# A Mamba block and a mixture of experts on one core: the row numbers of a routed tile's scatter are copied at the end of that tile's work

## The chip, the core and the metric

The kernel runs on one core of a Trainium2 chip. Its engines work side by side and wait for each other by semaphores: TensorE (matmuls, PE in the profile), VectorE (DVE), ScalarE (ACT), GpSimd (POOL) and SyncE (SP, which issues DMAs). The metric is the device time of one execution in microseconds (us).

## What is computed

A state-space block is added to x, and then a mixture of experts. Only the second matters here:

```python
scores = softmax(x @ gate_w.T)                 # 2048 tokens, 16 experts
topk_w, topk_ids = lax.top_k(scores, TOP_K)    # TOP_K = 6
topk_w = topk_w / (topk_w.sum(-1, keepdims=True) + 1e-20)
...
def body(acc, ew):
    w13_e, w2_e, c_e = ew
    y = _swiglu(x, w13_e, w2_e)
    return (acc + c_e[:, None] * y, None)
out, _ = lax.scan(body, jnp.zeros_like(x), (w13, w2, combine.T))
out = out + _swiglu(x, sw13, sw2)              # the shared expert, for all tokens
```

`_swiglu(x, w13, w2)` is `silu(x @ g.T) * (x @ u.T) @ w2.T` with 512 columns of x and 352 columns inside. Everything is float32.

## The kernel before

The work comes in two parts. Up to about 500 us the state-space block runs; then the experts' tiles follow, 128 tokens each. The first 32 tiles (`NS`) are the shared expert's, in two halves, with tokens in their own order. From tile 32 on come the routed tiles: the tokens of one expert are gathered from a table in HBM, worked on, weighted and added to the output rows by an indirect DMA with addition, a scatter. In the profiled execution there are 104 of them, tiles 32 to 135, for 16 experts. Most of them run in a loop of four tiles per turn (`Fori`), each of which has one of four slots.

A float32 matmul is made of three: every operand is split in a high part (rounded) and a low part (the rest), and high x high, high x low and low x high are summed. So a tile `t` passes through these steps, with the names of the tiles in SBUF:

- GpSimd gathers its rows into `xt` by the numbers in `gid`; SyncE sends them through HBM (`token_quarters`, `xs`), VectorE turns them into a PSUM bank (L1432).
- ScalarE writes the high part `xh` (L911), VectorE the low part `xl` (L1439, function `x_low`); TensorE multiplies both with the expert's weights (`up`, L1794 and L1795).
- ScalarE makes the silu `sg`, VectorE `am`, the product with the token's weight (L1479, `multiply`). TensorE transposes `am` (L1805, three matmuls per tile, which run between the two halves of the next tile's `up`), ScalarE writes `ah` (L921), VectorE `al` (L1485), and TensorE multiplies with the second weights (`down`, L1814).
- ScalarE copies the result to `ys` (L927), and GpSimd issues the scatter `out_x<-ys,aid` (L1074), which reads `ys` and the row numbers in `aid`.

Row numbers move through three small tiles of four columns, one per slot: `gid` (for the gather, written seven tiles ahead, L1456), `mid` (L1462, `keep_ids`, three tiles ahead) and `aid` (for the scatter, L1468, `add_ids`). Each is a copy of 128 x 1 int32 on VectorE. `add_ids` of a tile waits, by `added` of its slot, until the scatter of the tile four earlier has landed, since that one reads the same column.

When an expert begins, both ScalarE and VectorE write the high part of a later expert's weights, ScalarE then issues the load of the next raw weights, and GpSimd writes the low part in one subtraction (L1046), behind which its next scatters stand. Each engine runs its instructions in the order in which the program gives them; no scheduler moves them.

Of the kernel before, what the change touches and what calls it, by code (L numbers as in the profile page):

```python
# [54 lines left out]
NS = 2 * TT  # L55
# [180 lines left out]
def mamba_moe(nc, x, ctxT, g_x, g_f, inT, convw, convb, xpT, dtwT, dtb, alog, dvec,  # L236
# [13 lines left out]
    with ExitStack() as ctx:  # L250
        def alloc(stack, name, shape, dt=F32):
            return stack.enter_context(nc.sbuf_tensor(name, shape, dt))
# [27 lines left out]
        place = alloc(ctx, "place", [P, E, HALF])  # L280
# [218 lines left out]
        def at_least(eng, s, v):  # L499

            if isinstance(v, int) and v <= 0:
                return
            eng.wait_ge(s, v)
# [3 lines left out]
        def apart(eng, s, v, who):  # L507

            at_least(eng, s, v)
            if not isinstance(v, int):  # L510
                eng.sem_inc(waited[who], 1)

        def through(t, s):

            return 16 * (t // 4 + 1) if isinstance(t, int) else 4 * t + 16 - 4 * s
# [31 lines left out]
        def tiles_but_12(eng):  # L547
            return eng.value_load(fours[0:1, 1:2], min_val=NS + E - 12, max_val=TILES - 12)
# [4 lines left out]
        def up_banks(t, s):  # L553

            return misc if isinstance(t, int) and t == 0 else banks[2 * s:2 * s + 2]
# [20 lines left out]
        def _(sp):  # L576
# [28 lines left out]
            def xproj(q, _):  # L605
                bank, m = use("xproj", 0, q)
                apart(sp, gone[bank], m + 1, "sp")
                sp.dma_start(c_d[bass.ds(q, 1)].rearrange("a n t -> (a n) t"), xd[CP:CP + DS, :]).then_inc(cd_stored, 16)
# [535 lines left out]
        def _(dve):  # L1144
# [283 lines left out]
            def turn(t, s4, m=None):  # L1428

                of_slot(dve, moved[s4], t, m, "dve")  # L1430
                dve.wait_ge(xh_done, t - 1)
                nc.vector.transpose(banks[4 + 2 * (s4 % 2)][:].rearrange("p (b r g) -> p g b r", g=G, r=Q),  # L1432
                                    xs[:, s4, :].rearrange("p (g b c) -> p g b c", g=G, c=Q)).then_inc(xt_turned, 1)

            def x_low(t, s):
                dve.wait_ge(xh_done, t + 1)
                at_least(dve, up_done, t - 1)
                source = xt[:, t % 4, 0:H] if isinstance(t, int) and t < NS else banks[4 + 2 * s][:]
                nc.vector.tensor_tensor(xl[:, s, :], source, xh[:, s, :], ALU.subtract).then_inc(xl_done, 1)  # L1439

            def plan_of(t):

                word = dve.value_load(meta[0:1, 1, bass.ds(t, 1)], min_val=0, max_val=NX * (NX + 1) * NR - 1)
                return dve.snap(word % NX), dve.snap(word // NX % (NX + 1)), dve.snap(word // (NX * (NX + 1)))

            def take_weight(t, s4, number, m=None):

                rows_in(dve, t, s4, m, "dve")
                at_least(dve, am_done, t - 3)
                nc.vector.tensor_copy(cc[:, s4:s4 + 1], xt[:, s4, bass.ds(H - 1 + number, 1)]).then_inc(cc_done, 1)  # L1450
# [4 lines left out]
            def gather_ids(t, s4, column=None):  # L1455
                nc.vector.tensor_copy(gid[:, s4:s4 + 1], lists[:, bass.ds(ids_column(t) if column is None else column, 1)]).then_inc(gid_done, 1)  # L1456

            def keep_ids(t, s4):

                apart(dve, gid_done, t + 1, "dve")  # L1460
                apart(dve, aid_done, t - 3, "dve")
                nc.vector.tensor_copy(mid[:, s4:s4 + 1], gid[:, s4:s4 + 1]).then_inc(mid_done, 1)  # L1462

            def add_ids(t, s4):

                apart(dve, mid_done, t + 1, "dve")
                apart(dve, added[s4], through(t - 4, s4), "dve")
                nc.vector.tensor_copy(aid[:, s4:s4 + 1], mid[:, s4:s4 + 1]).then_inc(aid_done, 1)  # L1468

            def multiply(t, s4):  # L1470
                s = s4 % 2
                dve.wait_ge(sg_done, t + 1)
                if isinstance(t, int) and t < NS:
                    weight = share_w[:, 0:1]
                else:
                    dve.wait_ge(cc_done, t + 1)
                    weight = cc[:, s4:s4 + 1]
                at_least(dve, am_turned, t - 1)
                nc.vector.scalar_tensor_tensor(out=am[:, s, 0:I], in0=sg[:, s, :], scalar=weight,  # L1479
                                               in1=up_banks(t, s)[1][:, 0:I], op0=ALU.mult, op1=ALU.mult).then_inc(am_done, 1)  # L1480

            def a_low(t, s):
                dve.wait_ge(ah_done, t + 1)
                at_least(dve, down_done, t - 1)
                nc.vector.tensor_tensor(al[:, s, :], banks[5][:, 0:IP], ah[:, s, :], ALU.subtract).then_inc(al_done, 1)  # L1485
# [11 lines left out]
            def next_weights(t, e):  # L1497

                with dve.If(e > 0):
                    apart(dve, raw_in, raws_of(e), "dve")  # L1500
                    apart(dve, down_done, t, "dve")
                    nc.vector.tensor_copy(w[:, bass.ds((e % 2) * 2 * WCOLS + WCOLS - SHARE, SHARE)],
                                          raws[:, bass.ds((e % 2) * FAR + WCOLS - SHARE, SHARE)]).then_inc(wh_done, 1)

            def beside(work, t):
                for kind, i in work.get(t, ()):
                    if kind == "x2":
                        x2_(NB - 1, i)
                    elif kind == "stats2":
                        stats2(NB - 1, i)  # L1510
                    elif kind == "nmr":
                        nmr_(NB, i)
                    elif kind == "rank":
                        rank_tokens(i // 3, i % 3)
                    elif kind == "place":
                        place_tokens(i % 2)
                    elif kind == "match":
                        match_choices(i // 2, i % 2)
                    elif kind == "gate2":
                        gate(NB - 2, i)  # L1520
                    elif kind == "gate3":
                        gate(NB - 1, i)
                    elif kind == "low":
                        low_piece(i // EARLY, i % EARLY)
                    elif kind == "count":
                        count_tiles(i)
                    elif kind == "experts":
                        number_experts(i)
                    elif kind == "tiles":
                        number_tiles(i)  # L1530
                    else:
                        fill_table(i)

            def tile(t, place, m=None, takes=True, gathers=True):

                def slot_of(d):
                    return (place + d) % 4

                def group_of(d):
                    return None if m is None else m + (place + d) // 4  # L1540

                s, static = place % 2, isinstance(t, int)
                plain = static and t + TAKEN < NS
                if not plain:
                    split, number, column = plan_of(t)
                if not static or t + 1 >= NS:
                    turn(t + 1, slot_of(1), group_of(1))
                a_low(t - 1, 1 - s)
                if static:
                    beside(DVE_AFTER_A, t)  # L1550
                if takes and not plain:
                    take_weight(t + TAKEN, slot_of(TAKEN), number, group_of(TAKEN))
                    keep_ids(t + TAKEN, slot_of(TAKEN))
                if not static or t + 1 >= NS:
                    add_ids(t + 1, slot_of(1))
                if static and t < NS:
                    for late in FIRST_ROWS.get(t, ()):
                        if late >= NS + 4:
                            dve.wait_ge(mid_done, late - 3)
                        gather_ids(late, late % 4)  # L1560
                elif gathers:
                    apart(dve, mid_done, t + TAKEN + 1, "dve")
                    gather_ids(t + AHEAD, slot_of(AHEAD), column)
                x_low(t + 1, 1 - s)
                multiply(t, place % 4)
                if not static or t >= PEELED:
                    next_weights(t, split)

# [31 lines left out]
            last = tiles_but_12(dve) + 11  # L1600
            for k in range(4):
                tile(last - 4 + k, 3 + k, looped, k < 2, False)
            a_low(last - 1, 0)
            multiply(last, 3)
            a_low(last, 1)


# [312 lines left out]
```

## Time and profile before

| | |
|---|---|
| Median of 3 runs | 1419.17 us (1418.41 to 1422.58) |
| Profiled execution, its own time | 1422.3 us |
| Its span, first to last instruction | 1420.5 us |
| TensorE, busy | 1307.5 us |
| GpSimd, busy | 944.7 us |
| VectorE, busy | 851.5 us |
| ScalarE, busy | 729.5 us |

The span is what the trace covers; the execution's own time is 1.8 us more. Busy times are sums over the whole span, in which the two parts of the kernel lean on different engines, so they don't say what bounds the routed tiles; the rows further down are therefore mostly of the routed tiles alone.

### The profile page before, as it was taken

The page shows a single profiled execution, that of the slowest core. Times are in us where ns is not written, and L with a number is a line of the kernel's source. Part 1 is how long each engine was busy: PE and PEld are TensorE (multiplying, and loading weights), DVE is VectorE, ACT ScalarE, POOL GpSimd, SP SyncE. Part 2 cuts the span into 40 slices and gives each one's busy share as a digit, 9 for nine tenths or more (in the row PEclk, how much of TensorE's full clock was granted, in tenths as well). Part 3 has the DMA queues.
Part 4 walks back from the last instruction along what each step waited for, and adds up shares of the span by engine and source line. Part 5 has one row for each costly group of instructions (what it writes and reads, how often), then busy time and mean ns, then how long its engine had stood idle before and what let it go on. Part 6 is the DMA issues. An engine that isn't in the chain of part 4 may idle for free.

```text
span 1420.5 us, 31069 instructions
## 1 busy us (share of the span) xinstructions
PE 1307.5 (92%) x8064; PEld 1175.1 (83%) x8065; DVE 851.5 (60%) x1570; ACT 729.5 (51%) x1317; POOL 944.7 (67%) x671
## 2 busy tenths in 40 slices
PE   7897998998988899999789999999999999999995
PEld 2676887887888789999678988888988898888895
DVE  5879888897989865653244444444444445444441
ACT  5898887988879554343233333333333333333331
POOL 0589898999888847888366556666556665556722
PEclk8899999998999999999999999999999999999999
DMA  4121122223242555655487878887878778877752
GB/s 138 34 73 38 54 68 97 68 68 97 69 130 61 145 142 105 141 100 129 92 246 209 213 185 214 219 213 210 216 181 220 214 199 221 210 191 212 203 134 37
DMA packets 136276, 205.91 MB, mean 145 GB/s; under 512 B 20496, under 2 KB 74384, under 8 KB 134016
## 3 DMA queue, kind: packets, MB, share of 16 engines
q1 hardware_dynamic: 101744, 102.33, 23.8%
q0 software_dynamic: 31024, 62.10, 23.6%
q10 hardware_dynamic: 3440, 40.63, 8.1%
q8 instruction: 36, 0.59, 0.2%
q14 instruction: 32, 0.26, 0.1%
HBM read 130.99 MB, written 76.25 MB: 146 GB/s over the span
## 4 chain that ended last, share of the span: by engine, by line
PE 33%; POOL 12%; issue 9%; DMA 8%; DVE 4%; ACT 2%; POOLq 1%; ACTq 1%; DVEq 0%
PE bank L1814 11%; PE bank L1794 9%; PE bank L1795 9%; DMA out_x<-ys,aid 7%; POOL token_lists L1086 6%; POOL w L1046 4%; PE bank L1805 2%; POOL out_x L1068 1%; DVE hs L1236 1%; ACT w L876 1%; PE bank L1704 1%; PE bank L1690 1%; DVE xl L1439 1%; DMA out_x<-ys 1%; POOLq L1091 1%
## 5 line engine op out<-in xcount | busy, mean ns | idle before, releaser
L1794 PE MATMUL bank<-w,xh 128*128 (+1 forms) x1088 | 365.3, 337 | 26.0 <-DVE xl L1439 24.5
L1008 POOL TENSOR_TENSOR hc<-hs,crow 128x512 f32<-128x512 f32 x254 | 322.1, 1302 | 91.8 <-DVE hs L1236 86.2
L1795 PE MATMUL bank<-w,xh 128*128 (+1 forms) x1088 | 351.3, 323 | 0.0
L1074 POOL DMA_INDIRECT out_x<-ys,aid x104 | 165.2, 1589 | 254.6 <-issue 226.4
L1236 DVE TENSOR_TENSOR_SCAN hs<-dA,bank 128x512 f32<-128x512 f32 x256 | 295.7, 1208 | 50.3 <-PE bank L1704 31.6
L1814 PE MATMUL bank<-w,ah 128*128 (+1 forms) x816 | 259.3, 399 | 15.3 <-DVE al L1485 15.3
L1485 DVE TENSOR_TENSOR al<-bank,ah 128x384 fp32r<-128x384 f32 x136 | 75.8, 558 | 294.9 <-ACT ah L921 279.7
L1794 PEld LDWEIGHTS bank<-w,xh 128*128 128x128 f32 x1088 | 204.7, 188 | 42.5 <-issue 34.3
L927 ACT COPY ys<-bank 128x512 f32<-128x512 f32 x136 | 79.9, 587 | 262.8 <-PE bank L1814 262.8
L1795 PEld LDWEIGHTS bank<-w,xh 128*128 128x128 f32 x1088 | 206.7, 190 | 4.5
L1814 PEld LDWEIGHTS bank<-w,ah 128*128 128x128 f32 x816 | 150.2, 189 | 44.0 <-issue 12.9
L1795 PE MATMUL bank<-w,xl 128*128 (+1 forms) x544 | 176.0, 323 | 0.0
L1794 PE MATMUL bank<-w,xl 128*128 (+1 forms) x544 | 175.9, 323 | 0.0
L921 ACT CAST ah<-bank 128x384 fp32r<-128x384 f32 x136 | 65.2, 480 | 210.7 <-PE bank L1805 210.3
L1690 PE MATMUL bank<-ident,hc 128*128 128x128 f32 x1024 | 161.4, 282 | 7.3 <-POOL hc L1008 4.7
L1704 PE MATMUL bank<-bdiag,duT 128*128 128x128 f32 x1024 | 164.5, 285 | 0.0
L840 ACT ACTIVATE dA<-delta,aneg 128x512 f32<-128x512 f32 x256 | 164.2, 711 | 0.0
L1814 PE MATMUL bank<-w,al 128*128 (+1 forms) x408 | 161.3, 395 | 0.0
L1046 POOL TENSOR_TENSOR w<-raws,w x15 | 144.1, 9608 | 0.4
L1704 PEld LDWEIGHTS bank<-bdiag,duT 128*128 128x128 f32 x1024 | 143.1, 202 | 0.0
L1690 PEld LDWEIGHTS bank<-ident,hc 128*128 128x128 f32 x1024 | 125.6, 146 | 9.9 <-POOL hc L1008 6.1
L1702 PE MATMUL bank<-ident,gt 128*128 128x128 f32 x512 | 107.5, 293 | 26.4 <-DVE hs L1236 21.9
(184 smaller groups left out, 1983.6 us busy)
## 6 DMA issues: line engine op xcount, KB each, us to landing
raws<-in_wall ACTq DMA_DIRECT2D x16, 2176.0 KB, 8.9
token_quarters<-xt SPq DMA_DIRECT2D x104, 256.0 KB
xs<-token_quarters SPq DMA_DIRECT2D x104, 256.0 KB, 3.2
crow<-c_rows SPq DMA_DIRECT2D x64, 256.0 KB, 3.3
xt<-token_rows_turned SPq DMA_DIRECT2D x32, 256.0 KB, 2.9
out_x<-ys POOLq DMA_DIRECT2D x32, 256.0 KB, 4.2
token_rows<-rowb SPq DMA_DIRECT2D x4, 1028.0 KB, 5.9
xrow<-in_x SPq DMA_DIRECT2D x4, 1024.0 KB, 8.0
```

Of the source, the lines that this page charges most:

```text
L840: nc.scalar.activation(dA[:, 4 * (n % 2) + j, :], delta[b % 2][:, j, :], ACT.Exp, scale=aneg[:, j, n:n + 1]).then_inc(dA_done, 1)
L1008: nc.gpsimd.tensor_tensor(hc[:, j, :], hs[:, j, :], crow[:, n % 4, :], ALU.mult).then_inc(hc_done, 1)
L1046: nc.gpsimd.tensor_tensor(columns(w, at + WCOLS, WCOLS), raws[:, raw_at(e)], columns(w, at, WCOLS), ALU.subtract).then_inc(wl_done, 1)
L1074: pool.indirect_dma_start(out_rows, bass.IndirectOffsetOnAxis(ap=aid[:, s:s + 1], axis=0), ys[:, s, :], None, bounds_check=TOKENS - 1, oob ...
L1086: pool.indirect_dma_start(list_d[:, :], bass.IndirectOffsetOnAxis(ap=posi[:, c:c + 1], axis=0), ids[:, chunk:chunk + 1], None).then_inc(li ...
L1236: nc.vector.tensor_tensor_scan(hs[:, j, :], dA[:, 4 * (n % 2) + j, :], dbu[j % 2][:], 0.0, ALU.mult, ALU.add).then_inc(scanned, 1)
L1690: mm = nc.tensor.matmul(ysum[t][:, cols], hc[:, j, t * P:(t + 1) * P], ident[:], start=n == 0 and j == 0, stop=n == DS - 1, is_transpose=T ...
L1702: mm = nc.tensor.transpose(dbu[j % 2][:, t * P:(t + 1) * P], gt[:, n % 2, t, j * P:(j + 1) * P], ident[:])
L1704: mm = nc.tensor.matmul(dbu[j % 2][:, t * P:(t + 1) * P], duT[b % 2][:, t, j * P:(j + 1) * P], bdiag[:, n % 2, t - COPIED, :], start=True, ...
L1794: nc.tensor.matmul(gate_bank[:, 0:I], xx, columns(w, off + ww + k * 2 * I, I), start=first, stop=last)
L1795: mm = nc.tensor.matmul(up_bank[:, 0:I], xx, columns(w, off + ww + k * 2 * I + I, I), start=first, stop=last)
L1814: mm = nc.tensor.matmul(banks[7][:], aa, columns(w, off + ww + W2AT + k * H, H), start=k == 0 and n == 0, stop=k == IK - 1 and n == 2)
```

## The change

`add_ids` is called in another place. Before, the iteration for tile `t` copied the numbers of tile `t + 1`, between `keep_ids` and `gather_ids`, ahead of `x_low(t + 1)`. Now it copies those of its own tile `t`, behind `multiply(t)`, and ahead of `next_weights(t)`. The function itself is the same, with the same waits.

```diff
                 if takes and not plain:
                     take_weight(t + TAKEN, slot_of(TAKEN), number, group_of(TAKEN))
                     keep_ids(t + TAKEN, slot_of(TAKEN))
-                if not static or t + 1 >= NS:
-                    add_ids(t + 1, slot_of(1))
                 if static and t < NS:
...
                     gather_ids(t + AHEAD, slot_of(AHEAD), column)
                 x_low(t + 1, 1 - s)
                 multiply(t, place % 4)
+                if not static or t >= NS:
+                    add_ids(t, place % 4)
                 if not static or t >= PEELED:
                     next_weights(t, split)
...
             a_low(last - 1, 0)
             multiply(last, 3)
+            add_ids(last, 3)
             a_low(last, 1)
```

On VectorE, one tile's iteration in the loop before the change, from `al` to the branch around the weights (the semaphores each instruction waits for stand in brackets; `added1` belongs to the scatter in slot 1, `mid_done` to `mid`):

```order
L1485 TENSOR_TENSOR al<-bank,ah 128x384 [waits down_done,ah_done]
L1450 ISA [waits am_done,gathered3]
L1450 COPY cc<-xt 128x1
L1462 COPY mid<-gid 128x1 [waits aid_done,gid_done]
L1468 COPY aid<-mid 128x1 [waits added1,mid_done]
L1456 ISA [waits mid_done]
L1456 COPY gid<-lists 128x1
L1439 TENSOR_TENSOR xl<-bank,xh 128x512 [waits up_done,xh_done]
L1479 SCALAR_TENSOR_TENSOR am<-sg,cc,bank 128x352 [waits am_turned,cc_done,sg_done]
L1499 REGISTER_ALU
L1499 COMPARE_AND_BRANCH
```

The same iteration with the change:

```order
L1485 TENSOR_TENSOR al<-bank,ah 128x384 [waits down_done,ah_done]
L1450 ISA [waits am_done,gathered3]
L1450 COPY cc<-xt 128x1
L1462 COPY mid<-gid 128x1 [waits aid_done,gid_done]
L1456 ISA [waits mid_done]
L1456 COPY gid<-lists 128x1
L1439 TENSOR_TENSOR xl<-bank,xh 128x512 [waits up_done,xh_done]
L1479 SCALAR_TENSOR_TENSOR am<-sg,cc,bank 128x352 [waits am_turned,cc_done,sg_done]
L1468 COPY aid<-mid 128x1 [waits added0,mid_done]
L1499 REGISTER_ALU
L1499 COMPARE_AND_BRANCH
```

The `aid` copy has moved from the place before `gid` and `xl` to the place after `am`, and since it is the current tile's it waits for `added0`, the slot before.

At the end of VectorE's program, behind the loop, the last tile had no copy of its own before the change:

```order
L1485 TENSOR_TENSOR al<-bank,ah 128x384 [waits down_done,ah_done]
L1479 SCALAR_TENSOR_TENSOR am<-sg,cc,bank 128x352 [waits am_turned,cc_done,sg_done]
L1485 TENSOR_TENSOR al<-bank,ah 128x384 [waits down_done,ah_done]
L250 UNCONDITIONAL_BRANCH
```

With the change it has:

```order
L1485 TENSOR_TENSOR al<-bank,ah 128x384 [waits down_done,ah_done]
L1479 SCALAR_TENSOR_TENSOR am<-sg,cc,bank 128x352 [waits am_turned,cc_done,sg_done]
L503 ISA [waits mid_done]
L1468 COPY aid<-mid 128x1 [waits added3]
L1485 TENSOR_TENSOR al<-bank,ah 128x384 [waits down_done,ah_done]
L250 UNCONDITIONAL_BRANCH
```

Here the copy stands between `am` and `al` of the last tile. The other engines' orders are the same before and with the change.

## Rows read from the trace of the kernel before

**Rows 1.** The page: span, and busy time of each engine.

```profile
span 1420.5 us, 31069 instructions
...
PE 1307.5 (92%) x8064; PEld 1175.1 (83%) x8065; DVE 851.5 (60%) x1570; ACT 729.5 (51%) x1317; POOL 944.7 (67%) x671
```

**Rows 2.** Windows: stretch, length, busy us by engine, TensorE clock, DMA share, GB/s.

```profile
736.00:1392.00 656.00, 630.82 (x3564) 579.31 (x3563) 308.24 (x801) 225.75 (x410) 386.38 (x210) 1.00 0.78 202
```

**Rows 3.** Waits of TensorE, 736 to 1392 us: total us, times, longest.

```profile
PE bank L1794 <- DVE xl L1439: 19.4, 16, 1.5
PE bank L1814 <- DVE al L1485: 5.7, 14, 0.5
```

**Rows 4.** Waits of VectorE, 736 to 1392 us.

```profile
DVE al L1485 <- ACT ah L921: 192.3, 99, 2.5
DVE aid L1468 <- DMA out_x<-ys,aid: 47.0, 26, 2.7
```

**Rows 5.** Chain that ended last, 853 to 880 us: start, length, what.

```profile
855.45 9.71 DMA out_x<-ys,aid
...
868.11 5.06 DMA out_x<-ys,aid
...
873.70 0.70 DVE xl L1439
...
874.59 0.42 PE bank L1794
```

**Rows 6.** Timeline of VectorE there: start, length, instruction, idle time before and its releaser.

```profile
865.29 0.15 DVE L1468 COPY aid<-mid 128x1 int32<-128x1 int32 x1 [1.15 <-DMA out_x<-ys,aid]
...
873.30 0.15 DVE L1468 COPY aid<-mid 128x1 int32<-128x1 int32 x1 [2.52 <-DMA out_x<-ys,aid]
873.59 0.15 DVE L1456 COPY gid<-lists 128x1 int32 x1
...
879.92 0.57 DVE L1479 SCALAR_TENSOR_TENSOR am<-sg,cc,bank 128x352 f32<-128x352 f32 x1
...
883.93 0.56 DVE L1485 TENSOR_TENSOR al<-bank,ah 128x384 fp32r<-128x384 f32 x1 [1.89 <-ACT ah L921]
```

**Rows 7.** Timeline of GpSimd there.

```profile
858.35 9.59 POOL L1046 TENSOR_TENSOR w<-raws,w  x1
...
889.28 1.59 POOL L1074 DMA_INDIRECT out_x<-ys,aid  x1 [3.36 <-issue]
```

**Rows 8.** Timeline of TensorE: transposes of `am`, one line per tile.

```profile
735.93 0.49 PE L1805 MATMUL bank<-ident,am 128*128 128x128 f32 x3
...
855.33 0.49 PE L1805 MATMUL bank<-ident,am 128*128 128x128 f32 x3
...
862.23 0.49 PE L1805 MATMUL bank<-ident,am 128*128 128x128 f32 x3
...
868.71 0.49 PE L1805 MATMUL bank<-ident,am 128*128 128x128 f32 x3
...
876.63 0.49 PE L1805 MATMUL bank<-ident,am 128*128 128x128 f32 x3
...
1354.52 0.49 PE L1805 MATMUL bank<-ident,am 128*128 128x128 f32 x3
...
1392.28 0.49 PE L1805 MATMUL bank<-ident,am 128*128 128x128 f32 x3
```

**Rows 9.** Timeline of TensorE: its two kinds of stop at this start.

```profile
858.14 0.72 PE L1814 MATMUL bank<-w,ah 128*128 x2 [0.38 <-DVE al L1485]
...
874.59 0.42 PE L1794 MATMUL bank<-w,xh 128*128 x1 [1.37 <-DVE xl L1439]
```

**Rows 10.** Line L1074, the scatters: from issue to landing.

```profile
DMA to landing us min/median/max: 3.4/5.2/10.1
```

**Rows 11.** Timeline of VectorE at the end.

```profile
1403.07 0.58 DVE L1479 SCALAR_TENSOR_TENSOR am<-sg,cc,bank 128x352 f32<-128x352 f32 x1 [1.37 <-ACT sg L916]
1406.22 0.56 DVE L1485 TENSOR_TENSOR al<-bank,ah 128x384 fp32r<-128x384 f32 x1 [2.57 <-ACT ah L921]
```

## The prediction

> **What bounds the kernel now.** I read the page's first lines to see which engine is full, then the table of windows and the waits of TensorE and VectorE over the loop of routed tiles, then the chain that ended last around one expert start, and last the single instructions there. The profiled execution has a span of 1420.5 us, TensorE is busy in 92% of it, GpSimd in 67% and VectorE in 60% [rows 1]. The change touches only the routed tiles, so I cut out the stretch from 736 to 1392 us, which holds routed tiles alone. There TensorE is busy 630.82 of 656.00 us at a granted clock of 1.00, VectorE 308.24 [rows 2]: TensorE is the bound, and what it does not do is at most 25.2 us. Its waits there are two groups, 19.4 us in 16 waits for `xl`, the low half of x, and 5.7 us in 14 waits for `al`, the low half of the product [rows 3]. VectorE has its own waits: 192.3 us for ScalarE's `ah`, and 47.0 us in 26 waits in which the copy that writes `aid` stands until an earlier scatter has landed [rows 4]. The first of these two is slack (VectorE has little to do), the second need not be.
>
> The chain that ended last joins the two. Around the expert start at 858 us it goes: a scatter issued at 855.45 us takes 9.71 us to land, the next one, issued at 868.11, takes 5.06; then come 0.70 us of `xl` at 873.70 and TensorE's first matmul of the next tile at 874.59 [rows 5]. On VectorE the same moment reads: the `aid` copy at 873.30 after 2.52 us of waiting, the `gid` copy at 873.59 and only then `xl` [rows 6, 5]. The wait for the scatter stands ahead of `xl` in VectorE's order, though `xl` does not need it. Why the scatter is late is seen on GpSimd: from 858.35 it works 9.59 us on the low part of the next expert's weights, and the scatter of the tile that finished meanwhile goes out behind it [rows 7]. Call that tile A (its scatter is the one at 868.11).
>
> **What the change moves.** It removes nothing and adds nothing: 104 copies of `aid` stay 104, no DMA is moved, and no queue of SP, ScalarE or GpSimd changes its order. One VectorE copy of 0.15 us with its wait goes from before `gid` and `xl` of one iteration of the loop to after `multiply` of the next one. Both the old and the new place wait for the same scatter, that of the tile four earlier, so the wait comes more than one whole tile later.
>
> *The wait at its old place.* How much of the 47.0 us does TensorE feel? TensorE's period shows it better than its idle rows, since a matmul that starts again after a stop also looks longer. The transposes of `am` come once a tile. Six of them in a row, from 1354.52 to 1392.28 us, are 37.76 us, so 6.293 us is a tile without a stop [rows 8]. From 735.93 to 1392.28 there are 99 periods in 656.35 us [rows 8]; without any stop they would be 99 x 6.293 = 623.0, so 33.3 us are lost. One part of it is the wait for `al` in the first tile of an expert: at the start shown the period is 862.23 - 855.33 = 6.90, which is 0.61 too long, while its idle row says 0.38 [rows 8, 9]; the stop costs 0.23 more than its row. For 14 such stops that is 5.7 + 14 x 0.23 = 8.9 us [rows 3], and the change doesn't touch them: they wait for ScalarE. The other 33.3 - 8.9 = 24.4 us belong to `xl`. As a check: 19.4 us in 16 waits and 16 x 0.23 for starting again are 23.1 [rows 3]. At the start shown it is two periods, 6.48 and 7.92 instead of 6.29, together 1.82 us [rows 8].
>
> *Does `xl` become early enough?* In the tile with the 2.52 us wait, VectorE could have gone on at 873.30 - 2.52 = 870.78 us. From the `aid` copy to the start of `xl` it takes 0.40 us and `xl` itself 0.70, so `xl` would end by 871.9; TensorE, which started at 874.59 after 1.37 us of idleness, was ready at 873.22 [rows 5, 6, 9]. 1.3 us are left over, so I count the whole wait as gone. In an ordinary tile the copy is taken from before `xl` too, which makes `xl` some 0.2 to 0.4 us earlier and buys nothing, as TensorE isn't waiting.
>
> *The wait at its new place.* The copy for the tile A+4 now stands behind `am` of that tile. `am` starts at 879.92 us today and would start 1.8 earlier, at 878.1; it takes 0.57 us, so VectorE comes to the copy at 878.7. The scatter of A has landed at 868.11 + 5.06 = 873.17 by then [rows 5, 6]. That is 5.5 us of slack. For the scatter with the 9.71 us landing, one tile earlier, it is more: it lands at 865.16, and its copy comes one period of 6.3 us before A+4's, at about 872.4 [rows 5, 8], which leaves 7.2. No landing in the trace took longer than 10.1 us [rows 10]. So I set the new wait at nothing; its upper bound is below, with the rivals. Behind the copy stand, in the same tile, VectorE's share of the weights at an expert start, then the turning of the next tile's x and `al`. Those now come 0.2 to 0.4 us later (the copy and its semaphore). `al` covers that: it starts after 1.89 us of idleness [rows 6], and 192.3 us in 99 tiles are 1.9 us on average [rows 4]. Without that cover it would cost up to 0.4 us in 104 tiles, 42 us.
>
> *Who needs the copy.* GpSimd's scatter of A+4 waits for it; it went out at 889.28 us [rows 7], after the tile's output had been copied, or 1.8 earlier without the stops, and the copy is there by 878.9. More than eight us are left. At the very end the last tile's copy stands between its `am` (1403.07 + 0.58 us) and its `al`, which waits 2.57 us for ScalarE anyway [rows 11]: no cost. If that cover were gone it would be 0.3 us once.
>
> **Sum.** The profiled execution took 1422.3 us, 1.8 more than its span; less 24.4 it would be 1397.9. It lies 3.1 us above the median of the runs shown, 1419.17, and the profile doesn't tell in which part, so I take the saving off the median: 1419.17 - 24.4 = 1394.8, **1394.8 us**, about 1.7% less.
>
> **A rule that speaks against it.** GpSimd's weight subtraction reads and writes SBUF for 9.59 us from 858.35 to 867.94, and VectorE's `aid` copy, from SBUF to SBUF, ran inside that time at 865.29, in 0.15 us, 0.13 after the scatter had landed [rows 5 to 7]. So the row says that VectorE waited for the scatter and not for a port. The Trainium skill, page "SBUF — State Buffer", section "Who interferes with whom", says that VectorE and GpSimd share one pair of ports as an exclusive lock, and that whichever of a VectorE copy in a two-port mode and a GpSimd instruction starts first keeps the other out for its whole length. By that rule, if it held for these one-element copies, the `gid` copy, which stays ahead of `xl`, would stop in the other's place, and the time would stay at 1419; by the rows the sum above stands.
>
> **Rivals.**
> 1. *The stop is inherited.* Something else ahead of `xl` stands as long as the `aid` copy did, the `gid` copy above all. Time: 1419.2. For it: `gid` is the same kind of copy, in the same place. Against it: at 873.59 it followed `aid` by 0.29 us with no wait of its own [rows 6], and the `aid` copy inside GpSimd's subtraction wasn't slowed. Chance 0.02.
> 2. *Half is given back.* With the stops gone, the tiles behind an expert start come closer together, and GpSimd, late by one subtraction, or ScalarE, late by its weights, holds up another tile's `al` or `xl`. The stop for `al` is 0.6 us; if each of 14 starts had one more such stop, it would cost 14 x 0.61 = 8.5 us, time 1403.3. Against it: VectorE's slack of 1.3 us ahead of `xl` and 1.9 ahead of `al`. Chance 0.06.
> 3. *Slower: the wait comes back at the new place.* If the scatter of A had not landed when VectorE reaches the copy behind `am`, VectorE would stop with the weights, the turning and `al` behind it, and TensorE would wait for `al`, its next input. It begins when a landing takes 5.06 + 5.5 = 10.6 us where it takes 5.06 today; 1.9 us more are covered by the idleness ahead of `al`, and another 1.7 (24.4 in 14) would have to be lost before the kernel is slower than now: from 14.2 us on. At 15 it would be 14 x 0.8 = 11 us more than now, 1430. Against it: 10.1 is the longest seen, and that belongs to the other scatter, with 7 us to spare. Chance 0.02.
>
> **How the numbers follow.** The forecast has the remaining 0.90. Its own range is 1391 to 1399: the three runs of before spread from 1418.41 to 1422.58, some 4 us, and the term of 24.4 is uncertain by 1.3 (the check gives 23.1). To hold the first part of rival 2 as well the range goes up to 1402. 0.3% of this kernel is 4.3 us, about what a measurement can tell from no change; rival 2 is still faster than that, so faster has 0.96, within 0.3% 0.02, slower 0.02.
>
> **What the changed profile would show.** VectorE's wait of `aid` for the scatter gone or a few tenths, and no such wait on the copy's new line; TensorE's wait for `xl` between 736 and the end near nothing; its wait for `al` still 14 or 15 stops of about 0.4 us; the period of a tile 6.29 everywhere but in the first tile of an expert, at about 6.9; the scatter out of the chain that ended last, and TensorE alone in it there. The prediction is wrong if `xl` still stops TensorE with `gid`, `mid` or ScalarE's `xh` named before it, if the waits for `al` grow in number or length, or if the scatters' landings grow towards 11 us and `aid` waits again.

## The result and the profile after

| | before | changed | |
|---|---|---|---|
| median | 1419.14 us (1418.41 to 1422.58) | 1395.24 us (1392.24 to 1396.48) | ratio 0.9826, 95% interval 0.9808 to 0.9844 |
| profiled execution, span | 1420.5 us | 1394.7 us | |

The change saves 23.9 us on the median, where 24.4 was forecast (1394.8 us). In what follows the lines of TensorE are one higher than before, since the changed program has one line more behind the loop: the transposes of `am` are L1806, the `down` matmuls L1815, the `up` matmuls L1795 and L1796. Numbers up to L1502 are as before; in the experiments lines put in move them by up to five.

The page's first lines of the changed kernel, answering to [rows 1]:

```profile
span 1394.7 us, 31071 instructions
...
PE 1301.3 (93%) x8064; PEld 1177.1 (84%) x8065; DVE 848.6 (61%) x1570; ACT 729.3 (52%) x1317; POOL 944.1 (68%) x671
```

The busy time of every engine is as before, to 0.5% or better, in a span 25.8 us shorter: what went is waiting. The windows table over the routed tiles, as [rows 2], and below it TensorE's and VectorE's waits there, as [rows 3] and [rows 4]:

```profile
734.00:1366.00 632.00, 626.28 (x3565) 581.15 (x3564) 303.38 (x802) 225.80 (x410) 388.30 (x210) 1.00 0.80 209
```

```profile
PE bank L1815 <- DVE al L1485: 5.7, 14, 0.5
```

```profile
DVE al L1485 <- ACT ah L921: 180.4, 99, 2.2
DVE bank L1432 <- issue: 88.9, 90, 2.4
DVE gid L1456 <- DVE mid L1462: 27.8, 96, 0.5
```

TensorE's 19.4 us of waiting for `xl` are gone altogether, and its 14 waits for `al` are what they were, 5.7 us. VectorE's 47.0 us for the scatter are gone too. In their place nothing long came: `gid` now follows `mid` directly and waits some 0.3 us for it, as the `aid` copy did before, and the turning of x (L1432) starts later, behind the copy.

The chain that ended last, 853 to 880 us, answers to [rows 5]. Its summary is TensorE alone, where the scatter and `xl` were:

```profile
by line: PE bank L1815 36.2%; PE bank L1796 29.9%; PE bank L1795 29.8%; PE bank L1806 4.9%
```

The timeline of TensorE's transposes, as [rows 8]; the expert start shown lies about 6 us earlier than before:

```profile
734.51 0.49 PE L1806 MATMUL bank<-ident,am 128*128 128x128 f32 x3
...
849.14 0.49 PE L1806 MATMUL bank<-ident,am 128*128 128x128 f32 x3
...
856.04 0.49 PE L1806 MATMUL bank<-ident,am 128*128 128x128 f32 x3
...
862.34 0.49 PE L1806 MATMUL bank<-ident,am 128*128 128x128 f32 x3
...
868.63 0.49 PE L1806 MATMUL bank<-ident,am 128*128 128x128 f32 x3
...
1366.66 0.49 PE L1806 MATMUL bank<-ident,am 128*128 128x128 f32 x3
```

Behind the start the periods are 6.90, 6.30 and 6.29, where they were 6.90, 6.48 and 7.92. Between the same two tiles as in the prediction (99 periods) lie 632.15 us, 24.2 fewer than 656.35. The other 1.6 us of the spans' difference lie ahead of this stretch (1.4) and behind it (0.2).

GpSimd and VectorE around the start, answering to [rows 7] and [rows 6]:

```profile
852.17 9.60 POOL L1046 TENSOR_TENSOR w<-raws,w  x1
861.93 1.59 POOL L1074 DMA_INDIRECT out_x<-ys,aid  x1 [0.17 <-issue]
```

```profile
858.22 0.15 DVE L1456 COPY gid<-lists 128x1 int32 x1 [0.28 <-DVE mid L1462]
...
871.61 0.57 DVE L1479 SCALAR_TENSOR_TENSOR am<-sg,cc,bank 128x352 f32<-128x352 f32 x1
872.09 0.15 DVE L1468 COPY aid<-mid 128x1 int32<-128x1 int32 x1
873.07 0.73 DVE L1432 STREAM_TRANSPOSE bank<-xs 128x512 f32<-128x512 f32 x1 [0.83 <-issue]
...
875.96 0.56 DVE L1485 TENSOR_TENSOR al<-bank,ah 128x384 fp32r<-128x384 f32 x1 [2.16 <-ACT ah L921]
```

The scatter of tile A is as late as ever: it goes out at 861.93, right behind the subtraction. This trace doesn't tell when it landed; if that took 5.06 us as before [rows 5], it was done at 867.0, and VectorE comes to its copy at 872.09: an estimated 5.1 us of slack, where 5.5 were forecast. What the trace does show is that the copy had no wait. `al` still has 2.16 us of idleness ahead of it. The longest landing of a scatter that the trace tells is 10.2 us now, against 10.1 [rows 10].

### The profile page after: what moved, and what is told of

Its sections match the earlier page's. It is cut to its first block, busy times and chain, and to the rows that moved or that the text cites. A ratio compares the mean times of both kernels' runs of the same rounds, so it can differ in the third digit from the quotient of the medians.

```text
span 1394.7 us, 31071 instructions
## 1 busy us (share of the span) xinstructions
PE 1301.3 (93%) x8064; PEld 1177.1 (84%) x8065; DVE 848.6 (61%) x1570; ACT 729.3 (52%) x1317; POOL 944.1 (68%) x671
## 4 chain that ended last, share of the span: by engine, by line
PE 49%; POOL 8%; issue 6%; DVE 4%; ACTq 2%; ACT 1%; DMA 1%; DVEq 0%; POOLq 0%
PE bank L1815 17%; PE bank L1796 13%; PE bank L1795 13%; POOL token_lists L1086 6%; PE bank L1806 2%; POOL out_x L1068 1%; DVE hs L1236 1%; PE bank L1705 1%; PE bank L1691 1%; DVE al L1485 1%; ACTq L878 1%; DMA xt<-token_rows,gid 1%; ACT ah L921 1%; ACTq L931 1%; PE bank L1703 1%
## 5 line engine op out<-in xcount | busy, mean ns | idle before, releaser
L1795 PE MATMUL bank<-w,xh 128*128 (+1 forms) x1088 | 363.9, 335 | 7.3 <-DVE xl L1439 5.9
L1796 PE MATMUL bank<-w,xh 128*128 (+1 forms) x1088 | 352.2, 324 | 0.0
L1074 POOL DMA_INDIRECT out_x<-ys,aid x104 | 165.3, 1589 | 229.1 <-issue 199.6
L1815 PE MATMUL bank<-w,ah 128*128 (+1 forms) x816 | 259.2, 399 | 14.0 <-DVE al L1485 14.0
L1795 PEld LDWEIGHTS bank<-w,xh 128*128 128x128 f32 x1088 | 205.2, 189 | 15.7 <-issue 5.9
L1796 PEld LDWEIGHTS bank<-w,xh 128*128 128x128 f32 x1088 | 207.4, 191 | 5.5
L1815 PEld LDWEIGHTS bank<-w,ah 128*128 128x128 f32 x816 | 150.1, 189 | 42.8 <-issue 13.0
L1796 PE MATMUL bank<-w,xl 128*128 (+1 forms) x544 | 176.5, 324 | 0.0
L1795 PE MATMUL bank<-w,xl 128*128 (+1 forms) x544 | 176.4, 324 | 0.0
L1815 PE MATMUL bank<-w,al 128*128 (+1 forms) x408 | 161.1, 395 | 0.0
```

The source lines that it names most:

```text
L1074: pool.indirect_dma_start(out_rows, bass.IndirectOffsetOnAxis(ap=aid[:, s:s + 1], axis=0), ys[:, s, :], None, bounds_check=TOKENS - 1, oob ...
L1795: nc.tensor.matmul(gate_bank[:, 0:I], xx, columns(w, off + ww + k * 2 * I, I), start=first, stop=last)
L1796: mm = nc.tensor.matmul(up_bank[:, 0:I], xx, columns(w, off + ww + k * 2 * I + I, I), start=first, stop=last)
L1815: mm = nc.tensor.matmul(banks[7][:], aa, columns(w, off + ww + W2AT + k * H, H), start=k == 0 and n == 0, stop=k == IK - 1 and n == 2)
```

## The experiments

The first four ran on one chip with before at 1421.57 us, the next three with before at 1422.99, the last two with before at 1419.53.

| run | median us | ratio to before (95%) |
|---|---|---|
| own tile's numbers, old place | 1396.66 | 0.9824 (0.9808 to 0.9841) |
| next tile's numbers, new place | 1395.75 | 0.9813 (0.979 to 0.9836) |
| before, half the subtraction | 1400.43 | 0.9844 (0.9819 to 0.9869) |
| changed, ScalarE's weights later | 1383.74 | 0.9745 (0.9718 to 0.9773) |
| changed, subtraction 1.5 times | 1401.03 | 0.9836 (0.9808 to 0.9864) |
| changed, subtraction twice | 1445.28 | 1.0153 (1.0124 to 1.0181) |
| before, ScalarE's weights later | 1496.33 | 1.0517 (1.0492 to 1.0541) |
| changed, again | 1395.6 | 0.9836 (0.9815 to 0.9858) |
| changed, ScalarE's weights later, again | 1385.68 | 0.9767 (0.9746 to 0.9788) |

### Place or tile: each half of the change alone

The change does two things: the copy stands at another place, and there it writes the numbers of one tile earlier. The first run takes only the second half:

```diff
                     keep_ids(t + TAKEN, slot_of(TAKEN))
-                if not static or t + 1 >= NS:
-                    add_ids(t + 1, slot_of(1))
+                if not static or t >= NS:
+                    add_ids(t, place % 4)
                 if static and t < NS:
...
+            add_ids(last, 3)
             multiply(last, 3)
```

> The copy writes the current tile's numbers, as in the change, but stands at the old place, ahead of gid and xl. Theory (the landing): xl was held by the late landing of a scatter and by nothing else; at the old place the current tile's copy waits for a scatter that was issued one tile earlier, so at the start shown VectorE comes to it at about 877 us where the scatter landed at 873.2, and there is no wait. 1395 us, 1392 to 1399. Rival (the place): the gain comes from taking the copy and its semaphore work off the way to xl, whatever it waits for; then this is the time of before, 1419 us.

1396.66 us, the whole gain. VectorE's timeline around the start shows the copy ahead of `xl`, without a wait for a scatter:

```profile
870.97 0.15 DVE L1468 COPY aid<-mid 128x1 int32<-128x1 int32 x1 [0.30 <-DVE mid L1462]
...
871.43 0.69 DVE L1439 TENSOR_TENSOR xl<-bank,xh 128x512 fp32r<-128x512 f32 x1
```

The 99 periods take 632.28 us, against 632.15 with the change. So a copy ahead of `xl` costs nothing; what cost was the landing of the scatter that it waited for. The second run takes the other half:

```diff
-                if not static or t + 1 >= NS:
-                    add_ids(t + 1, slot_of(1))
...
                 multiply(t, place % 4)
+                if not static or t + 1 >= NS:
+                    add_ids(t + 1, slot_of(1))
                 if not static or t >= PEELED:
```

> The copy writes the next tile's numbers, as before the change, but stands behind multiply, as in the change. Theory (the landing): VectorE still meets the late scatter, for about 1 us at each expert start (it comes to the copy at about 872.3, the scatter lands at 873.2), but behind it stand only the turning and al, which has 1.9 us of idleness to cover that; 1395 us, 1392 to 1399, with some 15 waits of 0.5 to 1.2 us of aid for the scatter in the rows and no stop of TensorE for xl. Rival (any stop of VectorE there is felt): al takes over the stop, 1405 to 1419 us.

1395.75 us, the whole gain again, with the wait still there. VectorE's waits, and its timeline at a start:

```profile
DVE aid L1468 <- DMA out_x<-ys,aid: 13.9, 16, 1.1
```

```profile
868.96 0.15 DVE L1468 COPY aid<-mid 128x1 int32<-128x1 int32 x1 [0.83 <-DMA out_x<-ys,aid]
...
871.74 0.56 DVE L1485 TENSOR_TENSOR al<-bank,ah 128x384 fp32r<-128x384 f32 x1 [0.26 <-ACT ah L921]
```

VectorE stops 0.83 us, and of the idleness ahead of `al` 0.26 us are left. Each half alone is enough, then. This one has almost no room left. The first has some 4 us, estimated as above: its copy comes at 870.97 us, and its scatter went out at 862.03. The change has about 5.

### What makes the scatter late

```diff
-                nc.gpsimd.tensor_tensor(columns(w, at + WCOLS, WCOLS), raws[:, raw_at(e)], columns(w, at, WCOLS), ALU.subtract).then_inc(wl_done, 1)
+                half = WCOLS // 2
+                nc.gpsimd.tensor_tensor(columns(w, at + WCOLS, half), raws[:, bass.ds((e % 2) * FAR, half)], columns(w, at, half), ALU.subtract).then_inc(wl_done, 1)
```

The second half of those columns isn't renewed, so this run leaves that part of the result out.

> The kernel before, in which GpSimd subtracts only the first half of the columns of a routed expert's low weights (the second half is left as it was; that part of the result is left out): 4.8 us for 9.6. Theory (the subtraction makes the scatter of tile A late): the scatter goes out some 2.4 us earlier, at 865.7 of the timeline shown, as soon as GpSimd's wait for all earlier scatters at an expert's start has ended, and lands at about 870.8, when VectorE comes to it; of the 24.2 us some 20 come back, 1399 us, 1396 to 1403; the first, short wait stays, since it is for the scatter of 9.7 us landing that was issued before the subtraction. Rival (the wait at the expert's start makes it late, or the DMA does): 1415 to 1419 us.

1400.43 us: 21 of the 24 us, with the order of before. GpSimd, VectorE and TensorE's wait for `xl` from 720 us on:

```profile
854.88 4.88 POOL L1047 TENSOR_TENSOR w<-raws,w  x1
862.59 1.59 POOL L1075 DMA_INDIRECT out_x<-ys,aid  x1 [2.83 <-DVE aid L1469]
```

```profile
867.87 0.15 DVE L1469 COPY aid<-mid 128x1 int32<-128x1 int32 x1 [0.73 <-DMA out_x<-ys,aid]
```

```profile
PE bank L1795 <- DVE xl L1440: 1.3, 4, 0.5
```

With half the subtraction the scatter goes out 7.71 us after the subtraction's start instead of 9.76 [rows 5, 7], and VectorE's long wait shrinks from 2.52 to 0.73 us. But GpSimd stood idle for 2.83 us ahead of the scatter. The row names VectorE's copy for it, but the scatter's own numbers had been copied several tiles earlier; in the program GpSimd waits there, at an expert's start, for all earlier scatters to land. So the subtraction is the cause of the last two microseconds, which are the ones that TensorE felt, and the wait at the start stands behind it as the next limit. That second reading comes from the program; no run took that wait away.

### How much room the new place has

The changed kernel, with part of the subtraction done twice (`WCOLS // 2` columns in one run, all in the other):

```diff
...
+                extra = WCOLS // 2
+                nc.gpsimd.tensor_tensor(columns(w, at + WCOLS, extra), raws[:, bass.ds((e % 2) * FAR, extra)], columns(w, at, extra), ALU.subtract).then_inc(low_extra, 1)
+                apart(pool, low_extra, e, "pool")
                 nc.gpsimd.tensor_tensor(columns(w, at + WCOLS, WCOLS), raws[:, raw_at(e)], columns(w, at, WCOLS), ALU.subtract).then_inc(wl_done, 1)
...
```

> The changed kernel, in which GpSimd subtracts the first half of the columns twice at each of the 15 expert starts (same result): about 4.8 us and a wait for the first subtraction more. Theory (slack at the new place 5 us): the late scatter of each start lands about 5.0 us later, just as VectorE comes to the copy (at the start near 852 us of the changed kernel it would land at 872.0, the copy is at 872.09); no stop of TensorE or a few tenths in some starts: 1396 us, 1393 to 1401. Rival (no slack, the kernel follows GpSimd): 15 x 5 = 75 us more, 1470.

1401.03 us at the median, 0.9836 of before, where the changed kernel has 0.9826 and 0.9836: the intervals overlap, and no loss can be told. VectorE has no wait for a scatter. TensorE's waits for `al` from 720 us on, first here and then in the changed kernel:

```profile
PE bank L1820 <- DVE al L1490: 10.9, 16, 2.0
```

```profile
PE bank L1815 <- DVE al L1485: 8.5, 16, 2.0
```

That is 2.4 us more, and the 99 periods are 2.7 us longer (634.87 against 632.15): 5 us of lateness cost next to nothing.

> The same with the whole subtraction done twice: 9.6 us and a wait more. Theory (slack of 5 us at the new place, then the cover of 2 us ahead of al): VectorE stops 4.7 us behind am at each start, al covers 2.2 of it, TensorE stops 2.5 to 3.3 us longer than now, in its wait for al: 15 x 3.2 = 48 us, 1443 us, 1425 to 1455. This is the slower rival of the prediction with its decisive point put on trial: behind 10.6 + 1.9 us from issue to landing the stop is felt. Rival (the wait at the new place is never felt): 1396. Rival (GpSimd can't keep up, gathers come late): over 1460.

1445.28 us, some 47 more than the changed kernel would have beside that before (0.9826 x 1422.99 = 1398.2), 3.1 per start. TensorE's and VectorE's waits from 720 us on:

```profile
PE bank L1820 <- DVE al L1490: 43.3, 31, 3.0
```

```profile
DVE aid L1473 <- DMA out_x<-ys,aid: 64.3, 15, 4.9
DVE bank L1437 <- DMA xs<-token_quarters: 45.0, 23, 3.3
```

The slower rival of the prediction comes true where it was said to: the wait is back at the new place, 4.3 us at each of 15 starts, and TensorE feels it as a longer stop for `al`. 10 us of lateness are felt, then. The third row wasn't expected: the gathers come late as well, and the turning of x waits for them.

Not all of the 3.1 us per start is waiting. At one start TensorE stops for `al` like this, and the window behind it reads:

```profile
888.90 1.11 PE L1820 MATMUL bank<-w,ah 128*128 x2 [2.07 <-DVE al L1490]
```

```profile
890.00:891.00 1.00, 1.00 (x4) 0.81 (x3) 0.51 (x2) 0.00 (x0) 0.69 (x2) 0.50 1.14 311
```

The granted clock is 0.50 from 889 to 892 us. It falls like that at 7 of the 15 starts. Their longest periods are 4.2 us above 6.29 on average, those of the other 8 starts 2.2; 0.4 of the difference is in the stops' rows (2.4 and 2.0 us). So the clock makes up an estimated 11 of the 47 us, 1.5 at each of the 7 starts, and without it 2.4 us per start are left. In the changed kernel it is 1.00 over the routed tiles, as its windows line shows.

### The stop that is left

At the start of an expert `al` still stops TensorE for 0.65 us. ScalarE runs its share of the weights there, 2.0 us, ahead of `ah`. This run calls it one tile later, between `gate_up` and `y_out`:

```diff
                     gate_up(t, s)
+                    next_weights(t - 1)
                     y_out(t - 1, (2 + k) % 4)
-                    next_weights(t)
...
             gate_up(last, 1)
+            next_weights(last - 1)
             y_out(last - 1, 2)
             next_weights(last)
```

> The changed kernel, in which ScalarE's share of the next expert's weights (2.0 us) is called one tile later, between gate_up and y_out, where it is idle for 2.5 us, and no longer ahead of ah. Theory: what is left of the stops at an expert's start is al waiting for ah, which waits for this cast, 15 x 0.65 us; it goes: 1386 us, 1383 to 1390. The subtraction and its scatter come some 3 us later and still land 2 us before VectorE wants them. Rival (the stop only moves): y_out or the scatter's new wait takes over, 1393 to 1400 us.

1383.74 us. Of the waits for `al` one is left, at the very end; ScalarE and GpSimd around a start:

```profile
PE bank L1816 <- DVE al L1486: 2.0, 1, 2.0
```

```profile
847.35 2.01 ACT L876 CAST w<-raws  x1 [0.77 <-issue]
...
849.26 0.58 ACT L927 COPY ys<-bank 128x512 f32<-128x512 f32 x1
```

```profile
849.82 9.60 POOL L1047 TENSOR_TENSOR w<-raws,w  x1 [3.16 <-ACT w L876]
```

The cast fits between the silu and `ys`; GpSimd starts its subtraction 3.16 us late, and the new place of the copy has room for that. But it is 11.5 us below the changed kernel's 1395.24, more than 15 x 0.65, and the two were not run side by side. So both were run again, next to each other, five executions each:

> The changed kernel once more, beside the next one on the same chip. 24 us less than before by the loop of routed tiles: 1395 to 1399 us, ratio 0.983.

> The changed kernel with ScalarE's weights one tile later, once more. If the 15 stops for al are all that it takes away, it is 9 to 10 us faster than the changed kernel beside it; if the part ahead of the routed tiles has gained as well (3 us earlier in the first profile), 12 to 13 us.

1395.6 and 1385.68 us: 9.9 apart. The profiles agree that these are the stops for `al`: 99 periods take 632.28 and 623.40 us, 8.9 less, and the first routed tile's stop of 0.9 us is gone too. In the first pair the same stretch was 8.5 us shorter; most of what was left lies ahead of it, a part that differs by 2 us between the two profiles of the changed kernel (its first transposes at 734.51 and 732.48 us). The three runs with this edit are the earliest there, by 1.9 us or more, 0.9 of which is that first stop; whether the edit has a part in the rest isn't shown. This version is the fastest here. The same edit was made in the kernel before:

> The kernel before, with ScalarE's weights one tile later, as in the run that took the stops for al out of the changed kernel. Theory (the change made the room for it): the stop for al goes (15 x 0.65 us less), but GpSimd's subtraction starts 3.2 us later and the scatter of tile A with it, and ahead of xl VectorE waits for it 3.2 us longer: 15 x 2.5 = 38 us more than before, some 1458 us, 1445 to 1465. Rival (the two stops are independent): 10 us less than before, 1410.

1496.33 us, 73 slower than before instead of the 38 expected. TensorE's wait for `xl`, one such stop, and the windows around it:

```profile
PE bank L1795 <- DVE xl L1440: 80.3, 15, 6.4
```

```profile
838.18 0.66 PE L1795 MATMUL bank<-w,xh 128*128 x1 [5.14 <-DVE xl L1440]
```

```profile
828.50:832.00 3.50, 3.50 (x23) 3.26 (x22) 0.77 (x3) 1.43 (x3) 3.33 (x2) 1.00 0.27 98
...
836.00:838.00 2.00, 0.00 (x0) 0.00 (x0) 0.97 (x4) 0.00 (x0) 1.65 (x2) 0.50 0.89 165
838.00:840.00 2.00, 1.82 (x6) 1.83 (x7) 1.20 (x2) 0.00 (x0) 1.59 (x1) 0.50 0.89 140
840.00:842.00 2.00, 2.00 (x9) 1.93 (x8) 0.00 (x0) 0.00 (x0) 0.98 (x1) 0.50 0.97 304
```

The stop grows to 5.35 us on average, as theory said in kind. What it missed is the clock: during the 5.14 us without a matmul the granted clock falls to 0.50, the lower of its two levels (1.2 instead of 2.4 GHz), and stays there until about 842 us. The 99 periods take 112.6 us more than 99 x 6.293, and only 80.3 are in the stops' rows; with 0.3 us per stop for starting again, as measured below, the clock adds nearly 2 us to each of 15 starts. These 28 us are most of the 35 by which the theory fell short; the stops also grew by 4.1 us each instead of 3.2. Neither the kernel before (its longest routed stop for `xl` 1.5 us) nor the changed one lost the clock there. So without the change the edit that gives 10 us costs 73.

## Why the prediction was right

- *The bound, and how much of the wait TensorE feels.* Right, and to 0.2 us in the profile: 24.2 us between the same two tiles, 24.4 forecast. Counting by the period of a tile, and not by the idle rows alone (19.4 us), was needed for that. The surcharge per stop was taken from one stop for `al`, 0.23 us; the 14 that are left bear it out (9.1 us over 99 x 6.293, 5.7 of them in rows: 0.24 each), while the 16 for `xl` cost 0.30 each beyond their rows (24.2 against 19.4), which is why the prediction's check came to 23.1 only. That the median agrees as closely (1395.24 against 1394.8) is in part luck: the executions of one kernel lie 4 us apart.
- *The stops for `al` stay.* Right: 14 waits, 5.7 us in both. The last experiment pair shows them to be ScalarE's weights, 9.9 us in all.
- *`xl` becomes early enough.* Right: no wait of TensorE for it remains among the routed tiles.
- *The new wait costs nothing.* Right: VectorE never waits there, with 5.1 us of slack where 5.5 were worked out. That it is slack, not absence, shows in the runs with more subtraction: 5 us later costs next to nothing, 9.75 us later 3.1 us per start. There rival 3 was right in kind and its price too low: 9.75 us of lateness and a landing of 5.06 are 14.8 us in its reckoning, which makes some 8 us more than the kernel before, and 22 were measured. Most of the 14 us between is what the lower clock costs at 7 starts, a term that the prediction doesn't have.
- *The copy makes later work on VectorE 0.2 to 0.4 us later, under cover.* Right: in the 37 tiles without a stop in either profile, counted from TensorE's transposes, the turning of x starts 0.39 us later, and `al` at the same moment as before; of its 192.3 us of idleness 180.4 are left.
- *The cause of the late scatter.* Right for the microseconds that counted, but incomplete: half the subtraction brought 21 of 24 us, and GpSimd's wait at an expert's start for all earlier scatters stands 2.8 us behind. The prediction didn't see that second limit; the sum didn't need it.
- *The inherited stop.* It didn't happen: `gid`, a copy from SBUF to SBUF, ran at 858.22 us inside GpSimd's subtraction (852.17 to 861.77), in 0.15 us. By the rule of the Trainium skill, page "SBUF — State Buffer", section "Who interferes with whom", whichever of a VectorE copy in a two-port mode and a GpSimd instruction starts first keeps the other out for its whole length. The trace doesn't show that for these copies of one element per partition; whether they ran in such a mode no run shows.

## What to carry over

An engine that runs in order makes everything behind a wait as late as that wait, so a small bookkeeping copy belongs where its wait has long been met, or where only work with idle time ahead of it stands behind. Two ways out served equally well here (wait for an older transfer, or stand behind the urgent work); doing both leaves the most room, and the next change used 3 us of it. Count a stop by the period of the loop, since the idle row leaves out what starting again costs, and look at the granted clock behind the longer stops.

## What the runs showed of the hardware

- A matmul engine that has stopped costs more than the stop: 0.23 us at one stop of some tenths (0.61 in the period, 0.38 in the row), 0.30 on average at stops of 1.2. In the run where it stopped for 5.14 us the granted clock was 0.50 as well, with matmuls 0.29 us apart instead of 0.16 for nearly 4 us; where it stopped for 2.07 us, in the run with twice the subtraction, the clock was 0.50 for some 3 us.
- A scatter with addition of 128 rows landed 5.2 us after its issue at the median of 104. In the kernel before, 14 took 8.5 to 10.1 us, and these are the 14 that were issued within 0.3 us of the load of the next weights; no other took more than 7. In the three runs where ScalarE's weights come one tile later the load is issued about 4 us or more behind a scatter, and the longest landings that the traces tell are 7.6, 7.3 and 7.2 us.
